# A four-stage transformer kernel: the last stage written out, gated biases carried by the weights, transfers and routing steps moved

## The reference

```
x = x + A(ln(x), ctx)   # 8 experts of 512 hidden, relu; top-2 by ctx @ Wg + bg, softmax weights
x = x + B(ln(x))        # 16 experts of 128 hidden, silu(x@W1.T + b1) * (x@W3.T + b3), @W2.T + b2;
                        # 4 experts out of the 2 best of 4 groups, sigmoid weights, x 2.5
x = x + C(ln(x), ctx)   # attention, 16 heads of 8, causal mask without the diagonal
x = x + D(ln(x))        # D(n) = n + 0.5 * (silu((ln(n)*gamma + beta) @ w1 + fc1_bias) @ w2 + fc2_bias)
                        # w1 (128 x 512) and w2 stored as int32 with scales
```

## Time and profile before

| | us |
|---|---|
| runs, median (lowest to highest) | 939.17 (934.89 to 939.89) |
| the profiled execution, its own time | 934.4 |
| its span in the trace | 932.6 |
| busy: PE | 799.3 (86%) |
| busy: PE's weight loads | 608.4 (65%) |
| busy: DVE | 643.1 (69%) |
| busy: ACT | 504.1 (54%) |
| busy: POOL | 400.3 (43%) |

### The profile page before, as it was taken

How to read it: one execution, slowest core, us unless ns; L and a number is a source line. 1 busy time by engine, 2 the same in 40 slices (tenths; PEclk the granted TensorE clock), 3 DMA queues, 4 the chain that set the end, 5 groups by cost and what they waited for, 6 DMA issues and landing times.

```text
span 932.6 us, 18423 instructions
## 1 busy us (share of the span) xinstructions
PE 799.3 (86%) x5525; PEld 608.4 (65%) x5580; DVE 643.1 (69%) x1911; ACT 504.1 (54%) x972; POOL 400.3 (43%) x461
## 2 busy tenths in 40 slices
PE   3369898999994998988599899789999999987886
PEld 3358687899973787866388688545555555545564
...
GB/s 307 352 103 60 136 254 245 196 199 103 53 35 87 58 80 300 59 35 63 40 65 135 69 48 25 56 96 132 144 141 117 125 167 130 121 59 4 30 22 34
DMA packets 96153, 104.56 MB, mean 112 GB/s; under 512 B 13401, under 2 KB 71145, under 8 KB 94780
## 3 DMA queue, kind: packets, MB, share of 16 engines
...
## 4 chain that ended last, share of the span: by engine, by line
PE 38%; issue 14%; POOL 7%; DVE 7%; DMA 1%; ACT 1%; DVEq 0%; POOLq 0%; ACTq 0%
PE y_ps L1996 3%; PE y_ps L1909 3%; PE hid_ps L1972 3%; PE hid_ps L1973 2%; PE hid_ps L1984 2%; PE hid_ps L1894 2%; POOL xr L625 2%; PE tr_ps L2055 2%; POOL yg L633 2%; PE hid_ps L1877 2%; PE tr_ps L2027 1%; PE y_ps L290 1%; PE y_ps L1911 1%; PE hid_ps L1879 1%; PE y_ps L292 1%
## 5 line engine op out<-in xcount | busy, mean ns | idle before, releaser
L625 POOL DMA_INDIRECT xr<-b_tokens,idx_sb x70 | 66.7, 953 | 114.4 <-DVE idx_sb L901 94.1
L1120 DVE TENSOR_TENSOR hl<-hid_ps,hh 128x512 fp32r<-128x512 f32 x78 | 53.8, 690 | 69.3 <-ACT hh L1484 68.3
L1282 DVE TENSOR_REDUCE negmax<-hid_ps 128x4 f32<-128x512 f32 x128 | 85.9, 683 | 11.2 <-PE hid_ps L1973 10.5
L1783 PE MATMUL y_ps<-region,hh 128*128 x312 | 83.6, 345 | 10.7 <-DVE hl L1120 10.4
L633 POOL DMA_INDIRECT yg<-a_rows,idx_a x64 | 61.0, 954 | 50.3 <-issue 50.3
L1229 DVE TENSOR_TENSOR zb<-hid_ps,sg 128x256 f32<-128x256 f32 x70 | 29.7, 424 | 73.8 <-ACT sg L1568 51.9
L655 POOL DMA_INDIRECT yg<-b_rows,idx_b x64 | 61.0, 954 | 44.1 <-DMA b_rows<-yo 26.7
L1478 ACT ACTIVATE zb<-hid_ps 128x512 f32<-128x512 f32 x78 | 46.4, 595 | 60.5 <-PE hid_ps L1763 60.3
L1562 ACT ACTIVATE sg<-hid_ps 128x512 f32<-128x512 f32 x70 | 41.7, 596 | 67.4 <-PE hid_ps L1879 60.6
L1909 PE MATMUL y_ps<-region,hh 128*128 x280 | 75.4, 347 | 0.6 <-DVE hl L1240 0.6
L1973 PE MATMUL hid_ps<-region 128*128 128x512 f32 x128 | 75.2, 589 | 0.0
...
## 6 DMA issues: line engine op xcount, KB each, us to landing
region<-k_strips SPq DMA_DIRECT2D x128, 64.0 KB
...
region<-hl SPq DMA_DIRECT2D x128, 64.0 KB
...
```

The source lines that it names most:

```text
L625: g.indirect_dma_start(xr[:, q % 3, j * RB:j * RB + w], None, src, bass.IndirectOffsetOnAxis(ap=rows.bitcast(U32), axis=0)).then_inc(x_got ...
L1282: v.tensor_reduce(negmax[:, s % 2, b, :], hid_ps[b % 2][:].rearrange("p (i k) -> p i k", i=HG), AX, ALU.max, negate=True).then_inc(c_max, 1)
L1783: t.matmul(y[:, c0:c0 + 2 * P], hh[:, n % 2, cs], w2a[:, bass.ds(e * (2 * FA) + c * 2 * P, 2 * P)], start=c == 0, stop=False)
```

## The change

**Biases of B.** The inputs `b_w1` and `b_w3` now hold the bias as their last weight row (row 127), and the last feature of the normalised tokens is written as the constant 1.0. The true last row of the weights comes as a new input `b_last`, is loaded over 127 partitions (254 KB for each of 8 pieces) and subtracted from rows 0 to 126 on DVE (the "fold", before ACT takes the high half); the router's weights `wgb` get the same subtraction. A normalised token sums to zero, so its last feature is minus the sum of the others. The bias matmuls L1876 and L1883, the row table `bias_rows2` and its two transfers are gone.

**Transfers.** The x loads of blocks 4 to 7 leave ACT's queue for SP's. They, `fill_a` and `nought` now stand behind a wait on SP for the first four gathers of slots; `k_strips` behind the first group. W2 of B is loaded before W1 and W3, and a raw split comes every fourth tile from n = 3 on (`split_step`: 3, 7, ..., 47) where it was every third (2, 5, ..., 29, then 41 and 44).

**Routing steps.** The tables of tiles get other numbers; in A's first half the steps of the second half's routing stand one to two tiles later, K/V steps two tiles later, so that the last stands in the second half. On POOL two pows go ahead of `scatter_a(4)` and the third gather ahead of a pow; the last tile of a half does `down_a` ahead of `up_a`.

**Stage D.** The loop is written out. Statistics of blocks 0 to 6 are taken in C at the steps DST, with their pows on POOL; block 7's stand in D's block 0. The halving with the bias moves from DVE to ACT (`halve`). The order of each engine's work in a block changes, as the diff and the last pair of lists show.

```diff
-        CMB = ((7, 11, 16, 21), (7, 11, 15, 19))
-        STT = ((8, 12, 17, 22), (8, 12, 16, 20))
-        APP = ((10, 14, 19, 23), (9, 13, 17, 21))
-        FWD = ((12, 16, 21, 25), (11, 15, 19, 23))
-        LOG = ((13, 17, 22, 26), (12, 16, 20, 24))
+        CMB = ((6, 9, 13, 18), (3, 7, 11, 15))
+        STT = ((7, 10, 14, 19), (4, 8, 12, 16))
+        APP = ((11, 13, 17, 20), (7, 11, 15, 17))
+        FWD = ((13, 15, 19, 22), (9, 13, 17, 19))
+        LOG = ((14, 16, 20, 23), (10, 14, 18, 20))
         SGM, GRP, MSK, PRE, TOP, POS, WTS, HOT, EID, INV, SLT = (
-            (26, 24), (27, 25), (28, 25), (28, 26), (31, 26), (29, 28), (33, 29), (34, 30), (37, 33), (36, 32), (38, 33))
+            (23, 20), (24, 22), (25, 23), (25, 24), (28, 23), (26, 25), (30, 27), (31, 28), (34, 31), (33, 30), (35, 31))
         CH, PAIRS = 4, 8
         ESC = 2
         KVB = (6, 7, 0, 1, 2, 3, 4, 5)
-        KAT, VAT = [4 * i + 7 for i in range(NB)], [4 * i + 9 for i in range(NB)]
+        KAT, VAT = [4 * i + 9 for i in range(NB)], [4 * i + 11 for i in range(NB)]
         B2A, B2B = (0, 2, 4, 6), (1, 3, 5, 7)
         CMB2 = (4, 7, 10, 13)
+        DST = (22, 23, 25, 26, 28, 29, 32)
...
+        for q in range(EB // EQ):
+            v = w2b[:, q * 2 * BT:(q + 1) * 2 * BT].rearrange("p (c s d) -> p c s d", c=EQ, s=2)
+            raw_src.append((b_w2[:, q * BT:(q + 1) * BT], v[:, :, 0, :], v[:, :, 1, :]))
...
+        FOLD = range(NRAW_A + EB // EQ, NRAW_B)
...
+                if k in FOLD:
+                    row = b_last[:, (k - FOLD.start) * BT:(k - FOLD.start + 1) * BT]
+                    sp.dma_start(last_row(k), bass.AP(row.tensor, row.offset, [[0, P - 1], [1, BT]])).then_inc(in_raw[raw_slot(k)], 16)
...
-            sp.wait_ge(bias_out, 48)
+            sp.wait_ge(bias_out, 32)
             sp.wait_ge(cleared, 1)
             sp.dma_start(brows[0:3, :], brow[:, 0:AW]).then_inc(bias_in, 16)
-            sp.dma_start(brows[3:6, :], brow2).then_inc(bias_in, 16)
             sp.dma_start(brows[6:9, 0:EA * P], brow[:, AW:]).then_inc(bias_in, 16)
+            sp.wait_ge(x_got[0], 16 * NT)
+            for b in range(BH, NB):
+                sp.dma_start(X[:, b * BT:(b + 1) * BT].rearrange("p (t d) -> p t d", t=NT),
+                             x[b * BT:(b + 1) * BT, :].rearrange("(t p) d -> p t d", p=P)).then_inc(in_x[BH], 16)
             sp.wait_ge(cleared, 2)
             for k in range(4):
                 fill_a(k * GA // 4, (k + 1) * GA // 4)
             sp.dma_start(nought.rearrange("p (c d) -> p c d", d=BT), spread(sg[:, 1, :], [0, NT], [1, BT])).then_inc(filled_a, 16)
-            sp.dma_start(k_img.rearrange("(n r) c -> n r c", r=4 * HD)[:, 3 * HD:, :],
-                         bass.AP(c_ones.tensor, c_ones.offset, [[0, STEPS * HG], [BT, HD], [1, BT]])).then_inc(k_done, 16)
...
+                if q == 0:
+                    sp.dma_start(k_img.rearrange("(n r) c -> n r c", r=4 * HD)[:, 3 * HD:, :],
+                                 bass.AP(c_ones.tensor, c_ones.offset, [[0, STEPS * HG], [BT, HD], [1, BT]])).then_inc(k_done, 16)
+                if q == GA + 1:
...
-                    pool.wait_ge(logits_a, NH2)
+                    pool.wait_ge(kv_mm, 2 * NB)
...
-            scatter_a(4)
             power(6, 7)
             power(7, 8)
+            scatter_a(4)
...
+            gather_a(2)
             power(0, NB + 1)
-            gather_a(2)
...
+                    if n == split_step(k) - 1 and k in FOLD:
+                        eng.wait_ge(in_raw[raw_slot(k)], raw_landed(k))
+                        rows = raw_buf(k)[0:P - 1, :]
+                        v.tensor_tensor(rows, rows, last_row(k), ALU.subtract).then_inc(folded, 1)
...
+                if n == SA + 9:
+                    eng.wait_ge(scat, 128 * BH)
+                    v.memset(wide[:, :, :, P - 1:P], 1.0)
+                    v.tensor_tensor(wgb, wgb, wg_last, ALU.subtract)
...
+                if tau in DST:
+                    stats_d(DST.index(tau))
...
-                    ln_stats(eng, link, blk(i, p, 1) * BT)
-                    low(0)
-                    write_back(eng, STAGE_D, i, p)
-                    low(1)
-                    apply_next(eng, STAGE_D, i, p, 1)
-                    low(2)
-                    low(3)
-                    low_next(eng, STAGE_D, i, p)
-                    eng.wait_ge(d_down, at(0, i, p, CD, CD + 4))
-
-                    v.tensor_scalar(accT[:, p, :], y_ps[p][:], b2d[:, 0:1], 0.5, ALU.add, ALU.mult).then_inc(acc_ready, 1)
...
+            apply_d(0)
+            low_x(0)
+            for b in range(NB):
+                if b + 1 < NB:
+                    apply_d(b + 1)
+                low_d(b, 0)
+                residual(b)
+                low_d(b, 1)
+                if b + 1 < NB:
+                    low_x(b + 1)
+                write_back(b - 1)
+                low_d(b, 2)
+                low_d(b, 3)
+                if b == 0:
+                    eng.wait_ge(x_updated, NB + 1)
+                    stats_d(NB - 1)
+            write_back(NB - 1)
...
-            eng.wait_ge(logits_a, 1)
-            for b in range(BH, NB):
-                load_x(b)
...
+            def halve(b):
+                eng.wait_ge(d_down, CD * (b + 1))
+                a.activation(accT[:, b % 2, :], y_ps[b % 2][:], ACT.Identity, bias=b2h[:, 0:1], scale=0.5).then_inc(acc_ready, 1)
+
+            high_x(0)
+            for b in range(NB):
+                hidden(b, 0)
+                if b:
+                    halve(b - 1)
+                hidden(b, 1)
+                if b + 1 < NB:
+                    high_x(b + 1)
+                hidden(b, 2)
+                hidden(b, 3)
+            halve(NB - 1)
...
-                t.matmul(z, pick[:, 1, :], brows[:, bass.ds(e * BT, BT)], start=True, stop=False)
-                t.matmul(z, xTh[:, r, js], bw1h[:, bass.ds(e * BT, BT)], start=False, stop=False)
+                t.matmul(z, xTh[:, r, js], bw1h[:, bass.ds(e * BT, BT)], start=True, stop=False)
...
-                t.matmul(z, pick[:, 1, :], brows[:, bass.ds(e * BT + BW, BT)], start=True, stop=False)
-                t.matmul(z, xTh[:, r, js], bw3h[:, bass.ds(e * BT, BT)], start=False, stop=False)
+                t.matmul(z, xTh[:, r, js], bw3h[:, bass.ds(e * BT, BT)], start=True, stop=False)
...
-                    up(0)
-                    up(1)
-                    eng.wait_ge(acc_ready, at(STAGE_D, i, p, 1, 1))
-                    back(1 - p)
-                    up(2)
-                    up(3)
-                    down(0)
-                    down(1)
...
+            up_d(0, 0)
+            up_d(0, 1)
+            for b in range(NB):
+                up_d(b, 2)
+                up_d(b, 3)
+                if b + 1 < NB:
+                    eng.wait_ge(xn_ready, NB + b + 2)
                     fwd()
-                    down(2)
-                    down(3)
-            eng.wait_ge(xTl_ready, NS * NB + 1)
-            eng.wait_ge(acc_ready, NB * NS + 1)
-            back(1)
+                down_d(b, 0)
+                back_d(b - 1)
+                down_d(b, 1)
+                if b + 1 < NB:
+                    up_d(b + 1, 0)
+                    up_d(b + 1, 1)
+                down_d(b, 2)
+                down_d(b, 3)
+            back_d(NB - 1)
...
-        "b_w1": g[B + "W1"].transpose(2, 0, 1).reshape(P, -1),
-        "b_w3": g[B + "W3"].transpose(2, 0, 1).reshape(P, -1),
+        "b_w1": np.concatenate([g[B + "W1"].transpose(2, 0, 1).reshape(P, -1)[0:P - 1], g[B + "b1"].reshape(1, -1)]),
+        "b_w3": np.concatenate([g[B + "W3"].transpose(2, 0, 1).reshape(P, -1)[0:P - 1], g[B + "b3"].reshape(1, -1)]),
+        "b_last": np.concatenate([g[B + n][:, :, P - 1].reshape(1, -1) for n in ("W1", "W3")], axis=1),
```

283 lines of the change are left out of this document (150 added, 133 removed).

## The result

| | median (lowest to highest), us |
|---|---|
| before | 939.53 (934.89 to 940.38), 4 runs |
| the change | 916.52 (914.48 to 917.18), 4 runs |
| ratio | 0.9761, 95% interval 0.9726 to 0.9797 |

Faster by 2.4 per cent, 23 us, where 63 were forecast (876, range 856 to 900): the sign is right, the size is not. The profiled execution took 914.48 with a span of 912.7.

The account below looks back on a forecast made before the run. PE was taken as the bound nearly everywhere, falling short in five places. Terms -8 -10 +0 -7 -13 -8.5 +4 -20.5 sum to -63: profiled 871.4, plus 4.8 carried over, 876 us; range 856 to 900.

Parts of the forecast that it names:

- Setup, -8: Setup: bulk transfers put behind the first gathers let PE start 8 us earlier (bounds -3 to -12).
- Rival 1: Setup and A's first half: deferred bulk delays raw loads, ACT's split waits, both gain 0; 894 us, chance 0.12.
- A, first half, -10: A's first half: reordered pows and steps recover half of some 19 us lost on PE (-15 to 0).
- A, second half, 0: A's second half: moved routing steps are the same instructions, a K/V step comes in; no change (-1 to +2).
- Turn, -7: Turn A to B: slot cast three tiles earlier, so 6.8 us of matmuls lie over the gathers (-8 to -5).
- B, first half, -13: B's first half: two bias matmuls fewer per tile (15.8) and earlier slots (6), 60 per cent taken (-5 to -20).
- Rival 2: B and C: GpSimd's gathers and DVE set the length; B gains 6 instead of 21.5, C +8; 895 us, chance 0.15.
- B, second half, -8.5: B's second half: bias matmuls removed save 0.45 us in each of the last 19 tiles (-4 to -15).
- C, +4: Stage C: statistics for D's first blocks move in, 8.3 us of DVE work, half charged (0 to +8).
- D, -20.5: Stage D: written-out loop with less DVE work takes 7.05 us a block, from 10.1 (-15 to -24).
- rival 3: Stage D: low halves still stand between ACT and PE; 9.3 us a block, D -6; 890 us, chance 0.12.
- Rival 4: Stage B: small PE waits lower its clock; half the tiles at the lower level end at 971 us, chance 0.03.

Follow-up runs that it names:

- e11: e3 with the deferred bulk transfers again ahead of the first gathers, and the old tiles for the routing steps in B's first half; 890.5 us.
- e8: e3 with the deferred bulk transfers again ahead of the first gathers, on a slower chip (kernel before: 1102 us there); 1063.4 us.
- e1: The change with each of the eight b_last loads written to 128 partitions instead of 127; 890.2 us.
- e3: The change with both repairs: b_last loads over 128 partitions, and K and V stores issued ahead of the row store on SP; 880.1 us.
- e15: e14 with the K/V steps back at the tiles of the kernel before; 878.5 us.
- e13: e3 with GpSimd's gather of group 5 ahead of the last two pows and block 4's scatters; 873.1 us.
- e16: e14 with the routing steps of A's second half back at the tiles of the kernel before; 872.2 us.
- e17: e14 with the second combine of A's second half at tile 11 for 9, the third at 14 for 13, dependent steps one to two tiles later; 868.6 us.
- e14: e13 with GpSimd's first pow of A's second half ahead of the third gather instead of behind it; 872.7 us.
- e12: e3 without the eight folds and their b_last loads, so stage B lacks the last feature's part; 879.6 us.
- e10: e3 with the old tiles for the routing steps in A, and two bias matmuls on zero rows put back in each B tile; 893.5 us.
- e9: e3 with only D's blocks 0 and 1 measured in C, other statistics taken in D two blocks ahead, on the slower chip; 1075.6 us.

## Why the prediction was wrong, point by point

- **Setup, -8:** right, -7.8. First gather at 34.68, transposes at 41.84, 7.2 us after the gather's start. The deferral undone costs 5.6 at first up in e11 (7.8 in e8); taken with what the bulk does in A's first tiles, the deferral is worth 3.9 (some 2 in e8). Rival 1, that the bulk bites back on ACT's raw split, did not happen: its one wait there is 0.8 us, at 61.22.
- **A, first half, -10 became +13.4:** the failed step is the sentence "Their eight loads of 254 KB lie beside work too." They were priced by their bytes. The row of the wait list and e1 show that they were to be priced by their shape: 127 partitions, about one engine's share, some 11 us each at 23 GB/s, with everything behind them on the queue: 14.7 of this half (142.1 to 127.4). A second step was missing: K/V steps two tiles later put the V store behind a row store that comes shortly before the next V copy; its order undone gives 9.7 more (e3). These two undone, the stage gives -11.0. That this meets the -10 is in part luck: 5.4 of it is the K/V steps' new place (e15), which the prediction did not price, and the reordering of GpSimd, which it did, left the gather of e13 late. The Trainium skill (DMA: Bandwidth & Descriptors, "Why a DMA increments its semaphore by 16 and not by 1") names the case: the copy goes over the largest number of engines up to 16 that divides the outer dimension, and for 127 partitions that is one. The 7.1% share of the trace, for 6.25% of one engine in 16, agrees.
- **A, second half, 0 became +24.4:** 12 is the slow loads (e1). Of the other 12, 10 is the turn's wait paid here (e16: 106.1), which the prediction missed: its step "the moved routing steps are the same instructions" prices their busy time, not the waits that they bring along. The combine ahead of its gathers is 4.7 of it (e17); which of the other steps hold the rest no run separates.
- **Turn, -7:** -10.2, but with the row above it nets to nothing (e14 against e16), and to -4.6 with the second combine later (e17 against e16).
- **B, first half, -13:** -12.6, a number met by luck, for its parts are others than named. Forecast were 15.8 of matmuls and 6 of slots at 60 per cent; measured are 0.6 for the matmuls (with the new steps in place) and 7.7 for the steps. About 4 is in neither. Rival 2's mechanism, chains that take what fewer matmuls give, is what happened to the matmuls here; its sign on GpSimd did not come, whose waits for variances in B fell from 22.1 us to 5.3.
- **B, second half, -8.5:** -5.3, and 5.0 of it by the matmuls, as reasoned. Tile by tile (e3 against e10) the first 13 tiles save 3.8, one wait behind them takes 4.1 back, and the last 20 save 5.3.
- **Folds on DVE at nothing:** right (e12).
- **C, +4:** +1.0 in all; by e9, 2 to 4 for five blocks' statistics.
- **D, -20.5:** -22.7. Pitch 6.68 for 7.05, and rival 3 did not happen. From 860 to 900 us PE is full, DVE and ACT are at about 90 per cent, and the clock is 1.00; before, it was 0.87 in the same stretch. Before, then the change:

```profile
860.00:900.00 40.00, 33.38 (x128) 23.43 (x128) 33.30 (x110) 25.50 (x38) 8.17 (x4) 0.87 0.09 26
```

```profile
860.00:900.00 40.00, 39.09 (x189) 30.49 (x188) 36.41 (x104) 35.33 (x59) 1.67 (x1) 1.00 0.12 34
```

- **Rival 4, a falling clock in B:** 0.94 and 0.95, for 0.93 and 0.95 before. It did not happen, with PE waiting 16 times for low halves.

The range began at 856 and ended at 900, since every term's worst case was worked out by how little it could gain; none had room for a new wait in A. e3, the change as it was meant, took 880.1, inside it, though A's second half and the turn together stood at +2.6 there where -7 was forecast.
